# Rows for expert tiles fetched and results stored by token, with a place-to-token map made on TensorE

## The reference

```python
# layer 0 ffn: 32 experts, top 1, plus a shared expert
scores = sigmoid(max(x @ gate_w)); xs = x * scores[:, None]
order = argsort(argmax(x @ gate_w)); sorted_x = xs[order]
d = grouped(silu(sorted_x @ gw[e]) * (sorted_x @ uw[e]) @ dw[e])
out = shared(x) + d[argsort(order)]
# layer 2 cond, layer 3 cond: 8 experts, top 2 of a sigmoid router, gelu, F = 256, plus shared experts
# layer 2 ffn: 8 experts, top 2 of a softmax, gated, F = 1024, plus shared experts
# layer 3 ffn: 16 experts, top 1, biased gelu, at most cap = 160 tokens each; a dropped token gets 0
```

## Time and profile before

| | |
|---|---|
| median of 3 runs | 1870.13 us (1861.41 to 1874.29) |
| profiled execution | 1879.61 us, span 1877.9 us |
| TensorE clock granted, mean | 0.895 |
| PE busy | 1508.4 us (80%) |
| DVE, ACT, POOL busy | 972.7, 660.2, 315.6 us |
| DMA | 213.18 MB, mean 114 GB/s |
| indirect transfers | 5 groups of writes (16, 32, 32, 32, 16), 5 of reads (16, 32, 32, 32, 16) |

### The profile page before, as it was taken

One profiled execution on the slowest core, in us unless ns is written; L12 is line 12 of the kernel. 1 busy time (PEld: TensorE's weight loads), 2 busy tenths in 40 slices (PEclk: granted clock), 3 DMA queues, 4 the chain that ended last, 5 costly groups with the idle time before them and its releaser, 6 DMA issues. The chain is left out here.

```text
span 1877.9 us, 26047 instructions
## 1 busy us (share of the span) xinstructions
PE 1508.4 (80%) x8186; PEld 1133.1 (60%) x8186; DVE 972.7 (52%) x1703; ACT 660.2 (35%) x981; POOL 315.6 (17%) x327
## 2 busy tenths in 40 slices
PE   3758787867679999887999999999965898518992
PEld 2533333633558777766788888887754776405662
DVE  2626677352353435463677777774542333325775
ACT  1327676211032333332555555553321232102110
POOL 0520000300034005143000000002407004230003
PEclk9979999887579999989999999999986999658996
DMA  6058982112042223025112222201122222136623
GB/s 195 17 207 314 353 314 76 57 53 91 2 156 101 68 88 118 25 79 221 45 58 104 90 90 88 113 15 51 57 90 97 93 89 87 34 111 242 236 104 109
DMA packets 75799, 213.18 MB, mean 114 GB/s; under 512 B 9696, under 2 KB 47984, under 8 KB 67472
## 3 DMA queue, kind: packets, MB, share of 16 engines
q1 hardware_dynamic: 52672, 152.20, 22.6%
q0 software_dynamic: 17952, 54.15, 8.6%
q10 hardware_dynamic: 5040, 5.11, 0.8%
HBM read 164.90 MB, written 46.53 MB: 113 GB/s over the span
## 5 line engine op out<-in xcount | busy, mean ns | idle before, releaser
L843 DVE TENSOR_TENSOR sb_h_split<-sb_big,sb_h_split 128x2048 fp32r<-128x2048 f32 x78 | 178.3, 2288 | 83.7 <-ACT sb_h_split L838 83.7
L838 ACT CAST sb_h_split<-sb_big 128x2048 fp32r x78 | 148.1, 1902 | 37.0 <-issue 36.0
L978 ACT COPY sb_g_space<-sb_big 128x1024 f32 x120 | 118.5, 1046 | 75.0 <-DMA sb_big<-in_l_routed 46.3
L978 DVE COPY sb_g_space<-sb_big 128x1024 f32 x168 | 108.4, 693 | 67.4 <-issue 38.8
L734 PE MATMUL ps<-sb_big,sb_e_hT 128*128 x624 | 141.0, 379 | 1.1 <-DVE sb_e_hT L887 1.1
L270 PE MATMUL ps<-sb_h_split 128*128 128x512 f32 x312 | 134.6, 432 | 8.7 <-DVE sb_h_split L862 5.9
L270 PE MATMUL ps<-sb_g_split,sb_g_ws 128*128 128x512 f32 x256 | 109.0, 426 | 28.5 <-DVE sb_g_product L449 17.4
L734 PEld LDWEIGHTS ps<-sb_big,sb_e_hT 128*128 128x128 f32 x624 | 118.2, 190 | 18.5 <-issue 1.3
L272 PE MATMUL ps<-sb_h_split 128*128 128x512 f32 x312 | 123.4, 396 | 0.0
L271 PE MATMUL ps<-sb_h_split 128*128 128x512 f32 x312 | 122.8, 393 | 0.0
L1014 PE MATMUL ps<-sb_g_space,sb_e_rT 128*32 128x512 f32 x768 | 97.1, 623 | 24.0 <-ACT sb_e_rT L1068 12.8
(11 more groups left out here) (387 smaller groups left out, 3232.5 us busy)
## 6 DMA issues: line engine op xcount, KB each, us to landing
sb_big<-in_l_routed SPq DMA_DIRECT2D x32, 1024.0 KB, 6.2
sb_big<-in_l2f_routed SPq DMA_DIRECT2D x8, 3072.0 KB, 11.4
sb_e_wring<-in_l_experts SPq DMA_DIRECT2D x16, 1408.0 KB, 6.4
sb_big<-in_l_routed SPq DMA_DIRECT2D x32, 512.0 KB, 7.3
sorted_out<-sb_big POOLq DMA_DIRECT2D x22, 512.0 KB, 4.5
sb_big<-sorted_in SPq DMA_DIRECT2D x18, 512.0 KB, 3.9
sorted_out<-sb_big SPq DMA_DIRECT2D x18, 512.0 KB, 2.9
sb_big<-sorted_in POOLq DMA_DIRECT2D x15, 512.0 KB, 10.6
```

Source lines behind the costliest of these rows:

```text
L838: act.copy(self.own[part][:, 0, :], self.raw(e, part)).then_inc(self.own_high[part], 1)
L843: dve.tensor_tensor(self.own[part][:, 1, :], self.raw(e, part), self.own[part][:, 0, :], ALU.subtract).then_inc(self.own_low[part], 1)
L978: last = copy(self.own[part][:, g, :], here.rearrange("p s n -> p (s n)"))
```

## The change

1. A map from place to token is made on chip. `mark` splits the place number of each token into tile (place shifted right by 7) and position in the tile, and writes two arrays: `marks` (token, tile) = token number where the tile is the token's, and `spots` (token, position) = 1 where the position is. `pe_trace` multiplies them, one product for each of the G = 16 or 32 groups of 128 tokens, summed in PSUM: the result holds at (position, tile) the token number, or 0 for an empty place. `rows_of` turns it into `in_row` and `out_row`.
2. Layer 0, layer 2 ffn and layer 3 ffn no longer scatter rows. The token rows are stored plainly by SP to a table `by_token`, and POOL gathers each tile's 128 rows from it (`GatheredRows`, 8 places deep, or 10 ahead in layer 3). The two cond halves still scatter to `sorted_in` and load lots (`LoadedRows`).
3. In all five places the results are written tile by tile by an indirect transfer to `results`, where they stand by token, and are loaded plainly by SP (`load_results`) instead of being gathered.
4. Layer 0: the up weights of the first four experts are loaded at the start of the half; POOL scales in place in `ctok`; the up ring moves to FCOL2 and EXTRA and the down ring to CTOK. In the experts' first round ACT copies rows before it fills, the down fill of a round comes inside its round, and the expert numbers are read from memory once a round and engine.

```diff
+            def mark(self, dve, link, q):
+                if q == 0:
+                    link(dve.tensor_copy(self.tall[:], self.slot[:]))
+                    link(dve.tensor_scalar(self.tall[:], self.tall[:], 7, None, ALU.arith_shift_right))
+                    link(dve.tensor_copy(self.high[:], self.tall[:]))
+                    link(dve.scalar_tensor_tensor(out=self.slot[:], in0=self.high[:], scalar=-float(P), in1=self.slot[:], ...))
+                link(dve.tensor_tensor(marks, lanes_iota[...], self.high[:, part]..., ALU.is_equal))
+                dve.tensor_tensor(marks, marks, ids[:, part]..., ALU.mult).then_inc(self.marked, 1)
+                dve.tensor_tensor(self.spots[:, part, :], lanes_iota[:]..., self.slot[:, part]..., ALU.is_equal
+                                  ).then_inc(self.marked, 1)
+            def pe_trace(self, pe):
+                self.wait_known(pe)
+                pe.wait_ge(self.marked, 8)
+                for n in range(self.G):
+                    last = pe.matmul(psum[:, 7, 256:256 + self.rounds], self.spots[:, n, :], self.marks[:, n, :], ...)
+                last.then_inc(self.traced, 1)
...
@@ pe_jobs: after the third up part of the second job, and before the first down
+                        if f == 2 and places is not None and n == n0:
+                            places.pe_trace(pe)
+                    if places is not None and n == n0:
+                        places.wait_rows(pe)
@@ dve_jobs, called with beside=trace
+                        def trace(m):
+                            if m < 4:
+                                places.mark(dve, link, m)
+                            if m == 6:
+                                places.rows_of(dve, link)
...
@@ GatheredRows, layer 0 and layer 2 ffn, on POOL
+            def serve(self, pool, outc, places):
+                for j in range(min(self.DEPTH, self.tiles)):
+                    self.gather(pool, j, places)
+                for j in range(self.tiles):
+                    pool.wait_ge(outc, j + 1)
+                    pool.indirect_dma_start(out=results, ...out_row..., in_=self.tile(j)).then_inc(...)
+                    n = j + self.DEPTH - 2
+                    if j >= 2 and n < self.tiles:
+                        pool.wait_ge(self.stored[n % self.DEPTH], 16 * (n // self.DEPTH))
+                        self.gather(pool, n, places)
...
@@ half_l0, SP
+                        def ready(sp):
+                            for c in range(NCH):
+                                sp.wait_ge(scaled, c + 1)
+                                sp.dma_start(chunk_of(by_token, c), ctok[...]).then_inc(written, 16)
+                            places.wait_known(sp)
+                            sp.wait_ge(written, 16 * NCH)
+                        experts.load_weights(sp, ready)
+                        line.wait_stored(sp)
+                        for c in (2, 3, 0, 1):
+                            load_results(sp, [ctok], c, got[c])
@@ half_l0, POOL
-                        scatter(pool, rows, rows0_in, places.slots, 1, sent)
-                        pool.wait_ge(sent, 16 * NT)
-                        line.serve(pool, experts.outc)
-                        line.wait_stored(pool)
-                        for c in (2, 3, 0, 1):
-                            gather_chunk(pool, rows0_out, places.slots, [ctok], c, got[c])
+                        pool.wait_ge(written, 16 * NCH)
+                        places.wait_rows(pool)
+                        line.serve(pool, experts.outc, places)
@@ half_cond (2 and 3), POOL: the scatter stays
                         scatter(pool, xtok, sorted_in, places.slots, 2, sent, glu, split)
-                        pool.wait_ge(experts.outc, experts.tiles)
-                        line.wait_stored(pool)
-                        for n, c in enumerate(chunk_order):
-                            gather_chunk(...)
+                        places.wait_rows(pool)
+                        line.scatter(pool, experts.outc, places)
@@ stage_sorted_biased, POOL
+                        for j in range(AHEAD):
+                            gather(j)
+                        for j in range(tiles):
+                            if j + AHEAD < tiles:
+                                gather(j + AHEAD)
+                            pool.wait_ge(outc, j + 1)
+                            pool.indirect_dma_start(out=results, ...out_row[:, j:j + 1]..., in_=rows[:, j, :]).then_inc(stored, 16)
@@ layer3 routing block: SP stores ctok to by_token; DVE and PE end with
+                        for q in range(4):
+                            places.mark(dve, link, q)
+                        places.rows_of(dve, link)
```

361 lines of the change are left out of this document (216 added, 145 removed).

## The result

The changed kernel takes 1824.07 us, median of 4 runs (1818.0 to 1827.92), against 1872.21 (1861.41 to 1876.08) for the kernel before in the same comparison: a ratio of 0.9728, interval 0.9689 to 0.9767. That is 48.1 us less, where 53.6 were predicted. Both kernels were run again later, more often: 1827.20 against 1875.11, ratio 0.9752 (0.9719 to 0.9785), 47.9 us less. The profiled execution of the changed kernel took 1827.07 us (span 1825.3, granted clock 0.905 in the mean).

What follows compares the result with a forecast made beforehand. No one engine was taken to bound the kernel; losses lay at joints where rows are scattered or gathered, and in starvation under POOL's unbroken indirect transfers. Terms -22.7 + 6 + 1 - 20 - 17.9 = -53.6 gave 1816.5 us, range 1780 to 1850.

Steps and rivals of the forecast that it cites:

- second pair: Layer 3 cond, second dense pair: without POOL's 32 gathers PE no longer starves, -30 us.
- R3: Rival: starvation isn't POOL's, any 4 MB of row traffic causes it; 4 us won, 1866 us; chance 0.12.
- (a): Layer 0 dense jobs: PE's down products, unstarved, end at 107.0 in place of 118.7, -11.7 us.
- (b): Layer 0: the trace product is new on PE's path, 32 passes by 0.11 us, +3.5 us.
- (c): Layer 0 expert start: weights loaded early, ACT copies rows first; 3.5 us after dense end, not 14.0: -10.5 us.
- R1: Rival: layer 0's rounds are bound by the weight stream, (c) doesn't carry, 10.5 us less won: 1827 us; chance 0.13.
- R2: Rival: layer 0 wins more, expert numbers read once a round, 24 rounds by 0.9 us: 1795 us; chance 0.11.
- (d): Layer 0, after the experts: gathers that starve PE give way to SP's plain loads, -4 us.
- Layer 3 cond, first pair, +10: Layer 3 cond before the experts: trace product, wait for `rows_of` and first down remain after the scatter, +10 us.
- Layer 3, -12.3: Layer 3 start, from places known: first expert product at 1678.5 in place of 1690.8, -12.3 us.
- R4: Rival: POOL's indirect transfers in the expert stages starve PE, 86 us and 68 us lost: 1971 us; chance 0.05.
- R5: Rival: POOL's writes at 3.30 us beside DVE bound cond tiles, 3.6 in place of 2.48 us: 1904 us; chance 0.03.

Runs made afterwards that it cites:

- the first pair of traces: Recorded profiles of the kernel before and the changed kernel, compared stage by stage; stage changes sum to -53.1 us, the changed kernel's profiled execution took 1827.07 us.
- the kernel with held gathers and the row on SP: Changed kernel, layer 0 gathering only two tiles before the dense downs are done and SP clearing the by-token table's empty row: 1819.33 us, ratio 0.9707.
- the late-weights kernel: Changed kernel, but layer 0 loads no expert weight before token rows are stored and the first dense job's downs are done: 1813.04 us, ratio 0.9885.
- the later pair: Profiles of the kernel before and the changed kernel taken later on one chip; stage changes sum to -41.3 us, medians 1875.11 and 1827.20 us.
- the second group: Four edits of the changed kernel on one chip: late weights, numbers read each fill, trace product twice, paused scatter; the kernel before takes 1834.63 us there.
- the gathered layer 3 cond: Changed kernel, but POOL gathers each tile's rows in layer 3 cond, eight ahead, in place of the scatter of 32 indirect writes: 1833.69 us.
- the one with pauses: Kernel before, but layer 3 cond's 32 gathers parted by three pauses after the 8th, 16th and 24th: 1856.92 us, ratio 0.9919.

## Why the prediction held, and where it didn't

**The whole.** 53.6 us were predicted and 48.1 measured, 47.9 in the later comparison. The mechanism behind half of it, POOL's unbroken indirect transfers starving the other engines in the second pair, was right and is now shown from three sides: it goes with the gathers (-26), it goes with mere pauses (-16.5, and what is left is a plain wait for the rows), and neither 4 MB from SP nor 32 plain transfers from POOL bring it back. R3 is out. The step "a short pause cures it" holds too. That the first pair of traces sums to -53.1 is in part luck. Its terms miss one way by 3.0 in layer 0, 1.5 and 2.8 before the experts of layer 2, 3.7 in the second pair, 2.8 and 3.6 in layer 3, and the other way by 6.6 and 3.8 in the tiles of the cond halves, 5.5 before layer 3 cond and 3.4 in its start.

**(a), layer 0.** Failed. The sum took "eight gathers, 10 us, is too short to starve it" from the 20 us of the long bursts. PE itself isn't starved by eight, but DVE is late behind them, and PE waits for DVE: the places-to-dense-end part shortened by 2.0 us, not by 8.2 (a and b together). Held back, it gives 3.9 more: DVE is 2.7 us late in the changed kernel, and PE's last downs, at a mean clock of 0.76, take 1.4 us longer. The rest, some 2 us, isn't starvation. In the kernel with held gathers and the row on SP, PE waits 1.38 us for DVE's split of the last job's hidden values (103 to 107, at full clock and with no transfer going), which the 11.5 us for 96 downs left out.

**(b), the trace products.** 3.65 us in layer 0 and 7.00 in layer 3 are as predicted. In the two-pick halves 64 passes take 8.7 to 10.2 us and not 7.0. The price of a pass was right at either clock: 0.11 us at 1.00 in layer 0 (24 columns), 0.22 at 0.50 in layer 3 (31 columns), and 0.19 in the window at 0.50 above (39 columns). What the sum missed is that these longer products don't keep the full clock to their end. Beyond its own time the low clock costs the next up part some 1.7 us more (8 of 24 products in 5 us), and PE then waits 1.65 us for `rows_of`. So both halves of layer 2 came out above their terms (+9.5 and +12.7 for 8, +6.8 and +6.7 for 4); the wait that ends last before each first tile wasn't followed in every run.

**(c), the weights.** The size was right, the reason for the most part wrong: the first round, turn to turn, went from 16.8 to 7.0 us (-9.8, predicted -10.5), but the late-weights kernel keeps all but 1.5 of it. What is left as the cause is that ACT copies the rows before it fills and that the down fill comes inside the round. Rounds 2 to 24 moved by 1 us in the first pair; a further 3.2 came off in the last round, which the text had not foreseen, and the kernel that reads the numbers in each fill gives exactly these back (17.4 for 14.2). In the later pair both stretches together moved by the same 4 us. R1 (nothing of c carries) is out, R2 (numbers once a round) is true for 4.2 of its 21 us, and for at most 8.3.

**(d) and the ends of the halves.** -4.5 and +0.5 in the two pairs for (d), -8.5 and -2.4 before layer 3 cond: the kernel before varies there by some 5 us from execution to execution, and the terms of 2 to 4 us can't be told from that.

**Cond tiles, 0.** Failed, on the good side: -3.6 and -4.0 in the later pair. I had read the pace of 2.48 as PE's own; it was 2.33 with one long tile in four, held up by the store of a lot. The further 3 us in layer 2 cond of the first pair were a low clock at its first tiles, which the later pair of profiles doesn't have.

**Layer 3 cond, first pair, +10.** +6.6 and +5.6: the trace product and `rows_of` lie in the shadow of the scatter more than I took. On the chip of the second group the scatter itself sets the end, and even a second trace product costs the half nothing.

**Second pair, -30.** -26.3 and -26.0. The starved side was read well (64 us; 65.9 from the first dense product to the end of the last). The other side, 34 us, was too short: PE needs 40.2 in the changed kernel with no "issue" idle in it. The sum of matmuls left out PE's wait of 4.27 us for DVE's split between the ups and the downs, and the low clock after it (0.50 from 1581.5 to 1586.5).

**Layer 3, -12.3.** -9.5 to the first row turn, -9.3 to the first product. Marks, trace and the change of block came as worked out (first gather at 14.1 us after the places, 14.9 predicted); the flight of the gathers, taken as 2.5 us, was 6.7 behind the four weight loads issued 0.7 us ahead of them.

**The end, -5.6.** -2.0 and -4.6. The gathers' time is gone, but the wait for the last scattered result takes 3 us of it back.

**R4 and R5.** Neither happened, both mechanisms exist. R4 is the tile stage of the gathered layer 3 cond, 0.7 us a tile lost. R5 is in the changed kernel's layer 2 ffn, in the view by line (xcount, busy us, mean ns, idle before it):

```profile
L593 POOL DMA_INDIRECT results<-sb_big,sb_s_out_row x38 | 103.9, 2733 | 298.4 <-ACT sb_big L824 298.4
```

The write beside DVE's splits takes 2733 ns in the mean, not 980. Of the 38, 35 begin 0.1 to 0.4 us after such a split (L898, 2.29 us, two inputs in SBUF) has begun, take 2.75 to 3.05 us and end 0.83 to 0.87 after it; one that begins 0.15 us before its split takes 0.97. A tile has 10 us here (8 in the prediction), so that is hidden. By the Trainium skill, "SBUF — State Buffer", section "SBUF: two separate sides", a DVE operation with two SBUF inputs and a POOL operation that reads SBUF lock each other out, and the one that starts first holds the ports for its whole length. These rows agree. The prediction cited the part of that section on operations that take both ports, and these splits are of the other kind.

**Is it late instructions?** The prediction took the idle time without a wait for a supply of instructions that runs dry. By the Trainium skill, "Runtime: NRT & Kernel Launch", section "Instruction fetch mechanics", supply is mostly hidden. PE's idle time without a wait is 18.6 us in the pair of one trace of the kernel before and none in the one with pauses, so whatever it is, it isn't hidden here. But the record speaks against blocks of instructions that come late. The page of the kernel before lists its DMA queues (packets, MB, share), among them

```profile
q8 instruction: 75, 1.23, 0.3%
```

which is one packet of 16 KB for 218 of PE's products and weight loads, so presumably PE's. In the view of the queues for 1574 to 1624, which holds the whole starved stretch, the only one is POOL's:

```profile
q0 software_dynamic: 1388, 3.79, 25.3%
```

PE is back at 2.82 us of 3 from 1613 to 1616, before the next packet of that kind (after 1624). So PE recovers without having been brought a block, as far as packets are recorded. "Starved" stands in this text for idle time without a wait; what holds the engines up meanwhile stays open.

**What stays open.** What in an indirect transfer holds the other engines up isn't known. Nor is why one chip starves so much less (first tile after 53 us in place of 64), nor where the kernel before saves its 27 to 40 us there: it wasn't profiled on that chip. The forecast was worked out from a trace that starves, and its 53.6 us hold for such a chip; on the other the gain is nearer 20.

## What to carry to other kernels

Look at how many indirect transfers are issued back to back, not at their bytes. Where the chip starves, eight made DVE some 3 us late, and what PE lost depended on whether it had to wait for DVE: 3.9 us in layer 0, 0.2 us of idle time without a wait under the twelves of layer 2 cond. Thirty-two cost 16.5 us over the same transfers with a pause of 2.3 us after every eight, made of clears that nobody needs. One indirect transfer beside 2.3 us of matmul work was free, two were not, so a gain from "gather instead of scatter" has to be worked out for the stage in which the transfers land. Put a tiny transfer on the queue that is idle, and keep narrow float32 products short, because the clock they lower is paid for by what comes after them. When a stretch is freed of one limit, look for the plain waits beneath it before adding up matmuls: they were the 4.3 and 1.4 us that this prediction missed.

## What the runs showed of the hardware

- Plain transfers issued by POOL (0.53 us each, 247 GB/s, DMA share 0.80) leave PE at 10.00 us of 10; indirect ones (1.28 us each, 105 GB/s, share 0.30 to 0.37) leave it 0.77 to 1.11 of 5 on a chip that starves.
- The starvation outlasts the issue of the transfers by some 4 us: POOL's last gather in layer 3 cond of the kernel before ends at 1609.4, PE is at 0.74 of 3 from 1610 to 1613 and at 2.82 of 3 from 1613 to 1616.
- No packet of instructions is recorded from 1574 to 1624 under that starvation, and PE recovers before the next one.
- The same code runs differently on different chips: 63.5 to 64.8 us against 53.2 to 53.7 for one stretch, and 1834.63 against 1861.21 and 1875.11 us for the kernel before.
- A trace product of 64 narrow passes ends at 1.2 GHz (16 passes in the 3 us from 546 to 549), and a second one right behind it runs at 0.50 (26 in 5 us), though PE is counted busy 5.00 of 5. One of 32 passes in 3.65 us stays at 1.00.
- An indirect write that begins just after a DVE operation with two inputs in SBUF takes 2.75 to 3.05 us and ends 0.83 to 0.87 us after it; one that begins first takes 0.97.
- Beside SP's stores of 0.5 MB a cond tile of PE takes 0.4 to 0.7 us longer (2.7 to 3.0 us in place of 2.3), with idle time but no wait; beside single tiles of 128 KB some 0.25.
